# Early row loads for tiles 5 and 6, and half of the list ends moved to ScalarE's queue

## What is computed

```
x = x + tanh(g_xattn) * attention(layernorm(x), ctx, ctx, bias)   # 16 heads, LoRA projections, bias per head
t = layernorm(x); e = argmax(t @ Wg + bg)                         # one of 8 experts for each token
x = x + tanh(g_ffn) * (gelu(t @ W1[e] + b1[e]) @ W2[e] + b2[e])
```

## Time and profile before

| | us |
|---|---|
| median of 3 runs | 1320.03 |
| lowest and highest | 1315.41, 1322.32 |
| the profiled execution, its own time | 1319.97 |
| its span, first to last instruction | 1318.1 |
| PE busy | 1271.6 |
| DVE busy | 1092.2 |
| POOL busy | 1033.2 |
| ACT busy | 859.0 |

### The profile page before, as it was taken

How to read it: one execution, slowest core, us unless ns; L and a number is a source line. 1 busy time by engine, 2 the same in 40 slices (tenths; PEclk the granted TensorE clock), 3 DMA queues, 4 the chain that set the end, 5 groups by cost and what they waited for, 6 DMA issues and landing times.

```text
span 1318.1 us, 42263 instructions
## 1 busy us (share of the span) xinstructions
PE 1271.6 (96%) x12820; PEld 1081.4 (82%) x12820; DVE 1092.2 (83%) x2504; ACT 859.0 (65%) x1915; POOL 1033.2 (78%) x1179
## 2 busy tenths in 40 slices
PE   8999999999999999999999999999997799999997
PEld 6888888888888888888888888888875588888886
DVE  6999999999999999999999999999998455555555
ACT  4777777777777777777777777777765233333332
POOL 5779898988888898889888898898887434454445
PEclk9999999999999999999999999999999899999999
DMA  7655565556555565565555555565543688888886
GB/s 242 223 173 187 183 198 182 180 184 198 190 177 181 186 200 177 181 187 197 186 182 188 197 176 182 188 199 182 177 160 100 209 250 265 273 269 267 262 258 195
DMA packets 110648, 263.47 MB, mean 200 GB/s; under 512 B 15332, under 2 KB 34278, under 8 KB 110464
## 3 DMA queue, kind: packets, MB, share of 16 engines
q1 hardware_dynamic: 97488, 227.32, 55.2%
q0 software_dynamic: 12624, 34.62, 6.8%
q10 hardware_dynamic: 480, 0.84, 0.2%
HBM read 226.72 MB, written 36.91 MB: 200 GB/s over the span
## 4 chain that ended last, share of the span: by engine, by line
PE 36%; DVE 22%; issue 22%; ACT 8%; SPq 4%; POOL 3%; DMA 3%; DVEq 1%; POOLq 0%; ACTq 0%
DVE sc L881 10%; PE bank L658 6%; PE bank L672 6%; PE bank L505 5%; PE bank L520 5%; PE bank L490 3%; ACT PT L745 3%; PE bank L552 3%; PE bank L608 2%; DMA xg<-rows_dram 2%; ACT KT L729 2%; DVE st L902 2%; DVE x L988 2%; PE bank L646 2%; DVE negmax L887 2%
## 5 line engine op out<-in xcount | busy, mean ns | idle before, releaser
L392 POOL TENSOR_TENSOR sc<-sc,negmax 128x1024 f32<-128x1024 f32 x256 | 482.2, 1901 | 32.3 <-DVE negmax L887 26.2
L881 DVE TENSOR_TENSOR sc<-bank,sc 128x512 f32<-128x512 f32 x512 | 328.1, 682 | 20.3 <-PE bank L490 18.9
L887 DVE TENSOR_REDUCE negmax<-sc 128x8 f32<-128x1024 f32 x256 | 312.4, 1220 | 16.9
L745 ACT ACTIVATE PT<-bank 128x512 f32<-128x512 f32 x512 | 278.5, 602 | 0.4 <-PE bank L505 0.2
L505 PE MATMUL bank<-cst,sc 128*128 128x128 f32 x2048 | 272.6, 276 | 0.0
L455 POOL DMA_INDIRECT out<-og,ids x135 | 133.6, 990 | 144.7 <-issue 134.7
L505 PEld LDWEIGHTS bank<-cst,sc 128*128 128x128 f32 x2048 | 225.3, 140 | 25.7 <-issue 25.3
L759 ACT COPY OT<-bank 128x512 f32<-128x512 f32 x128 | 75.1, 587 | 150.4 <-PE bank L552 150.4
L440 POOL DMA_INDIRECT rows_dram<-x2n,slot_i x128 | 136.4, 1066 | 31.9 <-issue 26.0
L490 PE MATMUL bank<-KT,QT 32*128 32x256 f32 x2048 | 147.6, 402 | 6.3 <-ACT x2T L781 4.8
L552 PE MATMUL bank<-PT,V 128*32 128x128 f32 x4096 | 137.9, 275 | 3.8 <-ACT PT L745 1.8
(11 more groups left out here) (133 smaller groups left out, 2040.3 us busy)
## 6 DMA issues: line engine op xcount, KB each, us to landing
sc<-in_bias SPq DMA_DIRECT2D x256, 512.0 KB
w_sb<-in_w SPq DMA_DIRECT2D x72, 257.0 KB
CT<-in_w SPq DMA_DIRECT2D x72, 256.0 KB
xg<-rows_dram SPq DMA_DIRECT2D x63, 272.0 KB
x_sb<-in_x SPq DMA_DIRECT2D x128, 128.0 KB, 2.1
CT<-in_ctx_in SPq DMA_DIRECT2D x64, 256.0 KB, 5.5
out<-og,ids POOLq DMA_INDIRECT x135
rows_dram<-x2n,slot_i POOLq DMA_INDIRECT x128, 4.2
```

Source lines behind the costliest of these rows:

```text
L392: nc.gpsimd.tensor_tensor(s, s, m, ALU.add).then_inc(sub_ok, 1)
L745: nc.scalar.activation(PT[:, t.slot(2), 512 * q:512 * q + 512], b_t[q % 2][:], ACT.Exp).then_inc(pt_ready, 1)
L881: nc.vector.tensor_tensor(s, b_s[q][:], s, ALU.add).then_inc(s_used, 1)
L887: nc.vector.tensor_reduce(negmax[:, t.slot(2), 8 * h:8 * h + 8], sc[:, t.slot(4), 1024 * h:1024 * h + 1024].rearrange("p (h k) -> p h k", ...
```

## The change

SP's first steps of the expert phase are written out: it loads the rows of tiles 0 to 6 and the weights of tiles 0 to 3, then waits for `s_tab` and writes list ends 0 to 3. Its steps begin at 2 instead of -3; steps 2 and 3 then have no rows to load, and the long wait stands at step 4 as before, ahead of the rows of tile 7. List ends 4 to 7 are written from ACT's queue, with the same waits: 4 and 5 between the copy of tile 2 and gelu 1, 6 and 7 behind gelu 1. No other engine's code changes.

```diff
--- before.py
+++ after.py
@@ -257,7 +257,7 @@
         LOOP = (2, N // U - 1)
         FIRST, LAST = -6, N + 8
         FLOOP = (1, TILES // FU - 1)
-        FFIRST, FLAST = -3, TILES + 1
+        FFIRST, FLAST = 2, TILES + 1
 
         block = ctx.enter_context(nc.Block())
 
@@ -281,6 +281,10 @@
             rounds, k = divmod(t.k, FU)
             per_round = (FU - t.slot(2)) * 16
             return t.i * per_round + rounds * per_round + k // 2 * (16 * HALVES)
+
+        def end_list(eng, e):
+            first = eng.value_load(tail_i[0:1, e:e + 1], min_val=0, max_val=DUMMY - FT)
+            eng.dma_start(rows_dram[bass.ds(first, P), :], vacant[:, 0:ROW]).then_inc(tail_out, 16)
 
         def norms_at(i, k):
 
@@ -343,38 +347,46 @@
             sp.wait_ge(v_ready, N)
             sp.wait_ge(tab_ok, 1)
 
+            def load_weights(t):
+                e = sp.value_load(tile_e[0:1, bass.ds(t.n(), 1)], min_val=0, max_val=EXPERTS - 1)
+                sp.dma_start(w1_sb[:, t.slot(4)], w1[e]).then_inc(w1_in[t.slot(4)], 16)
+                sp.dma_start(w2_sb[:, t.slot(4)], w2[e]).then_inc(w2_in[t.slot(4)], 16)
+
+            def load_rows(t):
+                b = sp.value_load(tile_b[0:1, bass.ds(t.n(), 1)], min_val=0, max_val=DUMMY)
+                m = halves(t)
+                sp.dma_start(xg[:, t.slot(8), 0:m].rearrange("p a r -> p (a r)"),
+                             rows_dram[bass.ds(b, P * m), :].rearrange("(p a) r -> p (a r)", p=P)
+                             ).then_inc(xg_in[t.slot(8)], 16)
+
             def fstep(i, k):
                 t = tile(i, k, -2)
                 if t:
                     if t.reached(4):
                         sp.wait_ge(y_ready, t.n(1, -3))
                         sp.nop(nofuse=True)
-                    e = sp.value_load(tile_e[0:1, bass.ds(t.n(), 1)], min_val=0, max_val=EXPERTS - 1)
-                    sp.dma_start(w1_sb[:, t.slot(4)], w1[e]).then_inc(w1_in[t.slot(4)], 16)
-                    sp.dma_start(w2_sb[:, t.slot(4)], w2[e]).then_inc(w2_in[t.slot(4)], 16)
-                if isinstance(i, int) and k == EARLY - 3:
-                    for q in x2_out:
-                        sp.wait_ge(q, 16 * (N // 8))
-                    sp.wait_ge(vacant_out, 16)
-                    sp.wait_ge(tail_out, 16 * EXPERTS)
-                    sp.wait_ge(tab_ok, 2)
+                    load_weights(t)
                 t = tile(i, k, -3)
-                if t:
+                if t and t.reached(EARLY):
                     if t.reached(8):
                         sp.wait_ge(og_ok, t.n(1, -7))
                         sp.nop(nofuse=True)
-                    b = sp.value_load(tile_b[0:1, bass.ds(t.n(), 1)], min_val=0, max_val=DUMMY)
-                    m = halves(t)
-                    sp.dma_start(xg[:, t.slot(8), 0:m].rearrange("p a r -> p (a r)"),
-                                 rows_dram[bass.ds(b, P * m), :].rearrange("(p a) r -> p (a r)", p=P)
-                                 ).then_inc(xg_in[t.slot(8)], 16)
-                if isinstance(i, int) and k in (1, 2):
-                    sp.wait_ge(s_tab, 4)
-                    sp.wait_ge(vacant_ok, 3)
-                    for e in range(4 * k - 4, 4 * k):
-                        first = sp.value_load(tail_i[0:1, e:e + 1], min_val=0, max_val=DUMMY - FT)
-                        sp.dma_start(rows_dram[bass.ds(first, P), :], vacant[:, 0:ROW]).then_inc(tail_out, 16)
-
+                    elif not t.reached(EARLY + 1):
+                        for q in x2_out:
+                            sp.wait_ge(q, 16 * (N // 8))
+                        sp.wait_ge(vacant_out, 16)
+                        sp.wait_ge(tail_out, 16 * EXPERTS)
+                        sp.wait_ge(tab_ok, 2)
+                    load_rows(t)
+
+            for k in range(EARLY):
+                load_rows(At(0, k, FU))
+                if k < 4:
+                    load_weights(At(0, k, FU))
+            sp.wait_ge(s_tab, 4)
+            sp.wait_ge(vacant_ok, 3)
+            for e in range(4):
+                end_list(sp, e)
             run_steps(sp, FFIRST, FLAST, FU, FLOOP, fstep)
             for n, q in enumerate(og_out):
                 sp.wait_ge(q, 16 * (FU - n) * (TILES // FU))
@@ -825,7 +837,13 @@
                 step(0, k)
             gelu(early[0])
             copy_rows(early[2])
+            act.wait_ge(s_tab, 4)
+            act.wait_ge(vacant_ok, 3)
+            end_list(act, 4)
+            end_list(act, 5)
             gelu(early[1])
+            end_list(act, 6)
+            end_list(act, 7)
             run_steps(act, 2, FLAST, FU, FLOOP, fstep)
 
         @block.vector
```

## The result

The changed kernel takes 1313.71 us (median of 12 runs, 1310.95 to 1318.63) against 1320.26 us for the kernel before (12 runs, 1315.41 to 1325.39): a ratio of 0.9948, 95% interval 0.9936 to 0.996. It is 0.52% faster, and the interval stays clear of 1. I had said that 0.5% can be told from no change; the ratio is just past that, and the interval lies on both sides of it. The forecast was 1312.0 us in a range of 1308.5 to 1319.2, with 0.50 on faster. The profiled execution took 1312.52 us, its span is 1310.6.

A forecast was written before the change was run, and what follows sets the result against it. TensorE (PE), busy 96% of the 1318.1 us span, was taken as the bound. From 1319.97 us, 2.41 + 4.02 + 1.67 = 8.10 us won at the hand-over gave 1311.9, forecast 1312.0, range 1308.5 to 1319.2.

The forecast's parts named there:

- Rows 5 and 6 up front: SP's queue: both loads out by about 1028.5, ending PE's waits; 2.41 us won at tile 5, 4.02 at tile 6.
- The clock: PE, tile 6 to tile 7: 1.67 us lost to the lower clock behind the wait is taken back, bounds 0 and 1.67.
- The late signals: PE's 1.23 us wait before the second product of tile 2 may go or stay: taken as 0, bounds 0 and 1.4.
- the three terms: PE's hand-over: 2.41 us at tile 5, 4.02 at tile 6 and 1.67 from the clock, sum 8.10.
- The list ends on ACT: ACT's queue: 1.17 us per list end, hidden behind PE's products at no cost; thinnest cover 0.8 us, on copy 3.
- The second half's worth: With list ends 4 to 7 left on SP, weights 5 leave 4.67 us later and PE loses about 3 of 8.1.
- Nothing given back: After the hand-over PE sets the pace, so the lead stays: 0 us given back, bound 0 to 8.1.
- 1, the late signals vanish by the change: Second product of tile 2 starts at 1040.83, another 1.4 us won: 1310.6 us; chance 0.10.
- 2, ACT's ends at the slow price: ACT's list ends take 2.16 us each, copy 3 comes 3.14 late; middle 1315.4 us; chance 0.15.
- 3, transfers set the pace: List ends and weights 5 share the DMA engines, so weights 5 come 3 us late: 1315.0 us; chance 0.12.
- 4, nothing arrives: The phase behind, paced by 267 GB/s, eats the lead, or early loads go out late: 1319.5 us; chance 0.10.
- 5, ACT as the bound: ACT's list ends hold PE; at 5.4 us each it costs 6.6 us more: 1327 us, slower; chance 0.03.

The follow-up runs named there:

- run 3: The changed kernel with all eight list ends on ACT, four before and four behind gelu 1; 1317.76 us, 0.9979 of the kernel before.
- run 9: The kernel before, unaltered, looked at again in the last session; 1311.68 us (one run), no ratio.
- run 1: The changed kernel with list ends 4 to 7 given back to SP, behind the weights of tile 4; 1315.76 us, 0.9961 of the kernel before.
- run 2: The kernel before with list ends 4 to 7 on ACT, rows 5 and 6 in their old places; 1316.84 us, 0.9973 of the kernel before.
- run 4: The changed kernel with SP issuing the weights of tiles 4 and 5 before its four list ends; 1314.86 us, 0.9968 of the kernel before.
- run 5: The changed kernel, unaltered, measured again in the third session on another chip; 1308.62 us, 0.9952 of the kernel before.
- run 12: The changed kernel with the rows of tiles 0 to 2 loaded ahead of the first weights; 1305.69 us, 0.993 of the kernel before.
- run 11: The changed kernel with 320 empty instructions on GpSimd ahead of its last four row scatters; 1308.79 us, 0.9947 of the kernel before.
- run 10: The changed kernel with GpSimd holding tile 0's result scatters until tile 1 is added up; 1306.92 us, 0.9944 of the kernel before.

## Why the prediction was right, point by point

**Rows 5 and 6 up front: right.** They left within 2.6 us of rows 4 (out by 1029.3, where I had said before 1030), and no tile waits for them. Measured from the second product of tile 2, tile 5 comes 1.83 us later instead of 4.14: 2.31 won, where I had put 2.41. From tile 5 to tile 6 it is 3.89 instead of 7.98: 4.09, where I had put 4.02. The 0.54 MB cost nothing that PE felt: tile 3's weights, named as what would be late if the cover failed, were not waited for.

**The clock: right.** Tile 6 to tile 7 takes 3.90 instead of 5.63 us: 1.73, where I had put 1.67. Runs 3 and 9 show the other side: behind waits of 3.61 and 3.21 us a group of eight matmuls took 3.78 and 3.08 us instead of 1.89.

**The late signals: taken as 0, and nearly so, by luck.** The distance from tile 3 to the second product of tile 2 grew by 0.33 us (7.66 to 7.99); my bounds of 0 and 1.4 allowed for a gain only, and should have been open at both ends. In runs 1, 2 and 4 it is 6.71, 7.23 and 7.36 us, with the late signals, and 6.27 to 6.28 in runs 5 and 9 without, so it could have come out 1.3 us lower for no doing of the change. With the three terms this gives the 7.80 us: 2.31 + 4.09 + 1.73 - 0.33.

**The list ends on ACT: right in price and in cover.** Two took 2.37 us ahead of gelu 1, 1.18 each where I took 1.17 from SP's second four, and two 1.76 ahead of copy 3; in run 3 it was 3.73 us for four (1036.76), and 4.66 for the next four. The price is not fixed: run 12 has 3.03 us for two ahead of gelu 1. The last of the four stands at 1039.22, past the 1038 that I had named, as ACT came to them 1.6 us later than in the sum. Copy 3 ended at 1039.31, wanted at 1040.44: 1.1 us of cover where 0.8 was forecast. Run 3 shows what comes when it is used up.

**The second half's worth: the sign right, the size by luck.** I had weights 5 some 4.67 us later without it, and PE losing about 3 of the 8.1. Weights 5 left 4.97 us later in run 1, and the hand-over was 3.25 us longer. But weights 5 cost only 2.28 of that; rows 7, which I had not counted and which also stand behind the ends, cost 2.25 more, and a shorter wait for gelu 2 hid 1.28. The true worth in this state is 4.53 us.

**Nothing given back: right, as far as can be told.** From tile 8 to the end 253.4 us against 254.5; two traces of the kernel before alone differ by 4.3 us there (254.5 and, in run 9, 250.2), so I don't count this one microsecond as part of the change, and a loss of the same size could not be seen there. The medians of the last session speak for none: 6.0 and 7.8 us in runs 11 and 10, against 6.43 in the hand-over.

**What was off** is the size by which it came out, 6.9 us by the ratio (1320.26 x 0.0052, interval 5.3 to 8.4) instead of 8.1. The sum had been made against one profiled execution, and in that one SP was held up (its first four ends took 7.06 us), which made rows 5 and 6 later than they are without this. Undisturbed, the terms are 1.35, 3.43 and 1.67 us (run 9 against 5), 6.4 together. Tile 8's transposes began at 1057.17 instead of 1055.5; that is not in the terms, which give 8.13, but in what lies ahead of them: tile 3 began 1.34 us later and the second product of tile 2 another 0.33. Whether single executions among the first twelve pairs were of the one kind or the other can't be seen from their times, so how far this explains the 1.2 us stays open; they also lie within the interval.

**The rivals.** 1, the late signals vanish by the change: no, they are there after it (1.54 us), and in the sessions where they are gone they are gone for both kernels. 2, ACT's ends at the slow price: no, 1.18 us or less, though SP's, beside them, took 6.41 us for four. 3, transfers set the pace: no; weights 5 left at 1044.20 and were there for the product at 1050.04, and when only their issue was put off (run 1) PE waited for them. The Trainium skill, page "DMA: Bandwidth & Descriptors", section "Issuing engines are not separate DMA queues", calls what one saves by spreading issues over engines usually small relative to the DMA itself. Here the trace does not agree: it was 3.25 us of hand-over (21.28 against 24.53), 4.53 without the part of gelu 2, since each of these DMAs costs its sequencer about a microsecond (4.16 us for four) and the next load waits behind four. 4, nothing arrives: no. 5, ACT as the bound: not with four ends; with eight (run 3) it is what PE waits for, and even that kernel stays below the one before, 0.9979.

## What to carry to other kernels

Where an engine waits for a transfer, look first at when the transfer was issued, and then at what stands ahead of it on the issuing queue: here DMAs that nobody was waiting for, at about 1 us of sequencer each, held up loads that were. Move them to a queue with slack, but count that slack from the rows and stop when it is used: four were free on ACT, eight cost 5 us of hand-over; and ask what waits for the moved transfers themselves (rows 7 in runs 1 and 4). A saving read from one execution should be read from a second one before its last microsecond is believed.

## What was not expected of the hardware

In six traces (before, changed, runs 1 to 4) signals from PE arrive late around the hand-over. It is no property of either kernel: the eight later traces, of the same two kernels and their variants, on another chip and on the same one, do not have it. In the trace of the changed kernel DVE shows it, too:

```profile
...
1043.03 0.40 DVE L1160 TENSOR_SCALAR tile_tab<-bank 1x242 int32<-1x242 f32 x1 [4.37 <-remote]
...
```

The product that this copy reads was issued on PE at 1038.06 and takes 0.38 us; DVE took it at 1043.03, with "remote" as the releaser, and ACT's gelu 2 starts at 1042.99. In the same stretch SP's four ends took 6.41 us (7.06 before, 6.26 and 7.69 in runs 1 and 2), and in the traces without it 3.64 to 3.92 (runs 5, 9 and 12). The stretch ends 0.9 us after GpSimd's sixth scatter in a row (1041.10 + 0.99) in the changed kernel, 1.3 us in the one before; but runs 5 and 11 have such a row of six, or eight, and no late signal, so the row of scatters alone does not make it.

It also begins earlier than that row. ACT's copy of the gate's products (LT) waits for a group of matmuls with `wg_pad`. The changed kernel, PE and ACT, and then run 5:

```profile
...
1024.63 0.80 PE L553 MATMUL bank<-x2T,wg_pad 128*32 128x128 f32 x16
...
1028.26 0.27 ACT L766 COPY LT<-bank 128x128 f32<-128x128 f32 x1 [3.68 <-issue]
...
```

```profile
...
1025.05 1.08 PE L553 MATMUL bank<-x2T,wg_pad 128*32 128x128 f32 x16
...
1026.20 0.27 ACT L766 COPY LT<-bank 128x128 f32<-128x128 f32 x1 [2.32 <-PE bank L553]
...
```

From the start of the group to the copy it is 3.63 us here and 1.15 there. In all eight traces without late signals it is 1.12 to 1.15, in the six others 2.14 (before), 3.63 (changed), 2.08, 2.96, 3.57 and 1.97 (runs 1 to 4). GpSimd's row of six begins only at 1034.23 in the changed kernel and at 1032.62 in the one before, so it is no cause of this one. And tile 3's 1.34 us come from here: the group itself began 0.55 us later than in the kernel before (1024.63 against 1024.08), the copy adds 1.49 (3.63 against 2.14), and 0.70 come back up to tile 3, as the products behind the copy take less (3.31 and 1.97 us instead of 3.76 and 2.23). In runs 1 and 4, which have the early rows as well, it was 2.08 and 1.97, so the change does not bring it.

The late signals were there in the first two sessions, and not in the last two, in which the kernel before was also 5.8 us faster (medians 1314.8 against 1320.6). Between two profiled executions of it, 3.2 us are in the hand-over (29.08 against 25.90) and 4.3 behind tile 8. What differed between these sessions I could not find out, and as it did not come back, moving GpSimd's outputs or PE's code was never tried against it. The change gains in both: 7.8 us of hand-over with the stretch, 6.4 without.
